# A new written order of the pieces, and new PSUM banks, in a transformer layer with routed experts

## The chip, the core and the metric

The kernel runs on one NeuronCore of a Trainium2 chip: one program, one launch. The time is the device time of the launch in microseconds (us), here the median of three runs. The core has five engines with a queue of instructions each: TensorE (PE in the profile; PEld is its weight load), VectorE (DVE), ScalarE (ACT), GpSimd (POOL) and SyncE (SP, which issues most of the transfers). Every engine takes its instructions strictly in the order written for it, and waits on semaphores for what the others make.

## The reference, cut to what matters

```python
h = layernorm(x) * (1 + ca) + sa                  # x: 8 x 1024 x 256, float32
q, k, v = split(h @ w_qkv)                        # 16 heads of 16
attn = softmax(where(causal, q @ k.T / 16, -1e30))
x = x + ga * ((attn @ v) @ w_o)
h = layernorm(x) * (1 + cb) + sb
shared = silu(h @ w1.T) * (h @ w2.T) @ w3.T       # hidden 1024
scores = sigmoid(h @ router_w.T)                  # 8 experts
gates = scores * (top 2 of scores + bias)
routed = sum over the 2 of  (silu(h1) * h2 * gate) @ w3[e].T
x = x + gb * (shared + routed)
```

`sa, ca, ga, sb, cb, gb` are six rows per batch element, made from `c` by a silu and a product with `wmod`.

## The kernel before, in words

The work is cut into **pieces**, and the order of all of them is written out by hand in the table `ORDER_OF` (from line 128): one list for each of the five kinds of batch, `first`, `second`, `loop`, `last` and `end`. The program runs `start`, then `first` (batch element 0), `second` (1), `loop` (2 to 6), `last` (7) and `end`. A batch computes the attention of element b and the shared feed-forward part of element b - 1; `end` computes the feed-forward part of element 7, all 71 expert tiles, and the output. `WORK` (line 336) holds the parsed lists. Each engine's program walks the same list (its function `batch`) and issues its own part of each piece, so that the list fixes the order on all five queues at once. It fixes nothing else: which semaphore a part waits for, and at which count, stands in the part's own function.

The pieces that the prediction speaks of, by name and number:

- `max:g:p` is the p-th of 18 blocks of q k products of a group of four heads, of which only the row maxima are wanted. TensorE (L1857) fills two PSUM banks, VectorE takes the maximum (`maxima`, L1338). For four of the 18 ScalarE copies the block (`copy_max`, L1130), GpSimd masks the copy (`select_max:g:p`, L941) and VectorE reduces it (`diag_max:g:p`, L1338). `shifts:g` and `max_turn:g` bring the maxima into the queries.
- `scores:t`, 80 a batch: TensorE (L1881) fills two banks, ScalarE takes the exponential (`exps`, L1148) into one of five buffers, which it must not write before `values:t-5` has read it; on the diagonal GpSimd masks it (L935).
- `values:t`: TensorE (L1903) adds up the products with v in one bank; `raw:n` and `normalise:n` finish a step on VectorE.
- `qk:g`, `v:h`, `turn:i`, `op:h`: projections and turns (L1831, L1843, L1819, L1981). `up:k:i` and `down:k:i` are the parts of the shared feed-forward (L1911, L1955), `hid:k` its way from fp32 to two fp16 halves.
- In `end`, for expert tile i (256 rows): `xr:i` lets VectorE work out gate and row numbers (L1550 to L1556), and lets SyncE issue the load of tile **i + 2** (`load_tile`, a transposing transfer at L740 and a small one at L742). `tup:i` is the tile's up projection: TensorE L1935, 24 matmuls into two banks, ScalarE's silu L1200, VectorE's product L1563. `tlo:i` splits the product (L1207, L1568). `ty:i` is the down projection: TensorE L1946, 12 matmuls into one bank, VectorE L1575, and two indirect stores by GpSimd (`add_tile`, L1017).
- Also in `end`: for each half m of a batch element `out_load:m` issues two loads on SyncE (base rows L754, 512 KB; the experts' sums L761, 1 MB), `out_make:m` is three VectorE operations of 128x1024 (L1581, L1590, L1592), `out_store:m` issues the store (L766). `out_load:0` waits for the stores of tiles 51 to 54; `out_load:m` from m = 2 on waits for `out_make:m-1` to be partly done, and from m = 4 on for `out_store:m-4` to have landed. `last_loads` and `out_end` do the same for the last four halves and wait for the last tiles.

PSUM has eight banks. `BANK_OF` (line 301) gives, as a row of digits for each kind of batch, the first bank of every use in the order of the list. The loop over `BATCHES` works out from it which earlier uses a piece's banks had last (`AFTER`), and TensorE's `take` (line 1809) waits until those were read (`was_read`, from line 1767). So a digit decides for which engine's work a piece waits.

## Time and profile before

| | us |
|---|---|
| median of three runs | 1887.2 |
| lowest and highest run | 1887.08, 1891.4 |
| the profiled execution, from its first to its last instruction (span) | 1884.2 |
| TensorE matmuls busy | 1724.3 |
| VectorE busy | 1581.7 |
| ScalarE busy | 1072.7 |
| GpSimd busy | 922.0 |

The profile is of one execution, whose own time is known only by its span. The median of the runs is 3.0 us above that span. Line numbers (L1881) are those of the kernel before. A matmul's end is modelled, so that two matmuls in a row seem to overlap; what a piece costs is better read as the distance from its first matmul to the first matmul of the next piece. The brackets at the end of a row give the idle time of the engine just before it, and what ended it.

### The profile page before, as it was taken

Reading aid. Unit: us, or ns where it says so; the run is one execution under the profiler, and the core shown is the slowest. Engines: PE = TensorE matmul, PEld = TensorE weight load, DVE = VectorE, ACT = ScalarE, POOL = GpSimd, SP = SyncE. Lnnn points to the kernel's source line nnn. Section 1 sums busy time; section 2 is a strip of 40 time slices with the busy share of each in tenths; the row PEclk is TensorE's granted clock in tenths of the full one; section 3 lists DMA queues with packets and bytes.
Section 4 is the critical chain, followed back from the end, with each engine's and each line's share of the span. In section 5 each row is a group of like instructions: output and inputs, shape, how many; then the busy total and the mean of one; then the engine's idle time right before and its main releaser. Section 6 shows DMA issues by size and latency. Waiting matters only on the chain. (4 is left out here: it accounts for less than half of the span.)

```text
span 1884.2 us, 46063 instructions
## 1 busy us (share of the span) xinstructions
PE 1724.3 (92%) x17630; PEld 984.1 (52%) x17630; DVE 1581.7 (84%) x2889; ACT 1072.7 (57%) x1346; POOL 922.0 (49%) x1003
## 2 busy tenths in 40 slices
PE   5677889999999999999999999999999998999987
PEld 2233435444554455445444545454545877778764
DVE  7999998898988898898889887988996676656787
ACT  2578767675766576667666765676575332323211
POOL 2233454455535554545545554545465376545423
PEclk8699999999999999999999999999999999999998
DMA  4236221303112312121212121213112775677998
GB/s 146 74 124 171 63 70 32 86 15 92 37 47 58 98 30 70 36 86 30 75 29 86 30 75 32 83 30 91 35 56 78 196 156 140 164 157 156 284 287 281
DMA packets 214132, 183.13 MB, mean 97 GB/s; under 512 B 146640, under 2 KB 182232, under 8 KB 212128
## 3 DMA queue, kind: packets, MB, share of 16 engines
q1 hardware_dynamic: 200768, 143.87, 29.6%
q0 software_dynamic: 12960, 36.06, 5.7%
q8 instruction: 146, 2.39, 0.5%
q14 instruction: 66, 0.54, 0.1%
q10 hardware_dynamic: 192, 0.26, 0.1%
HBM read 65.23 MB, written 62.19 MB: 68 GB/s over the span
## 5 line engine op out<-in xcount | busy, mean ns | idle before, releaser
L1148 ACT ACTIVATE arena<-pair 128x1024 f32<-128x1024 f32 (+1 forms) x640 | 569.3, 940 | 207.8 <-PE pair L1881 205.0
L1338 DVE TENSOR_REDUCE max_part<-pair 128x2 f32<-128x1024 f32 (+2 forms) x448 | 531.9, 1212 | 33.5 <-PE pair L1857 31.6
L1911 PE MATMUL pair<-feat_parts,ffn_sb 128*128 128x512 f16 x1536 | 379.4, 384 | 15.3 <-DMA feat_parts<-rows 5.0
L1903 PE MATMUL pair<-arena,v_sb 128*32 128x256 f32 (+1 forms) x5120 | 329.5, 368 | 5.1 <-POOL arena L935 1.0
L935 POOL TENSOR_SCALAR_AFFINE_SELECT arena<-arena 128x512 f32<-128x512 f32 x256 | 165.8, 658 | 265.7 <-ACT arena L1148 265.5
L1857 PE MATMUL pair<-arena 48*128 48x128 f16 (+3 forms) x2304 | 209.6, 282 | 39.8 <-DVE max_part L1338 14.7
L1881 PE MATMUL pair<-arena 50*128 50x256 f16 (+1 forms) x2560 | 208.4, 264 | 32.9 <-DVE silu_h L1386 7.9
L1911 PEld LDWEIGHTS pair<-feat_parts,ffn_sb 128*128 128x128 f16 x1536 | 133.7, 98 | 189.6 <-issue 38.5
L1017 POOL DMA_INDIRECT slots<-arena,feat x142 | 146.1, 1029 | 156.0 <-DVE arena L1575 127.5
L1023 POOL TENSOR_TENSOR hidden<-silu_h,hidden 128x512 f16<-128x512 f32 x128 | 149.8, 1172 | 147.7 <-ACT hidden L1181 147.0
L1935 PE MATMUL pair<-parts,arena 128*128 128x256 f16 x1704 | 201.7, 276 | 11.0 <-DMA parts<-lists 4.0
L941 POOL TENSOR_SCALAR_AFFINE_SELECT arena<-arena 128x1024 f32<-128x1024 f32 x128 | 141.7, 1107 | 127.5 <-ACT arena L1130 127.2
L1903 PEld LDWEIGHTS pair<-arena,v_sb 128*32 128x32 f32 x5120 | 130.6, 110 | 127.9 <-issue 64.0
L1955 PE MATMUL pair<-ffn_sb,hidden 128*128 128x256 f16 x1536 | 185.9, 274 | 3.2 <-POOL hidden L1023 3.2
L1935 PEld LDWEIGHTS pair<-parts,arena 128*128 x1704 | 166.6, 99 | 39.9 <-issue 15.5
L1881 PEld LDWEIGHTS pair<-arena 50*128 50x128 f16 x2560 | 86.9, 95 | 172.9 <-ACT arena L1148 43.4
L1857 PEld LDWEIGHTS pair<-arena 48*128 48x128 f16 x2304 | 83.5, 96 | 171.0 <-issue 43.5
L1955 PEld LDWEIGHTS pair<-ffn_sb,hidden 128*128 128x128 f16 x1536 | 145.4, 98 | 41.4 <-issue 14.5
L1130 ACT ACTIVATE arena<-pair 128x1024 f32<-128x1024 f32 x128 | 131.1, 1024 | 60.6 <-PE pair L1857 57.0
L1002 POOL DMA_INDIRECT lists<-rows,slot_now x128 | 127.4, 995 | 64.3 <-DVE slot_now L1482 35.5
L1338 DVE TENSOR_REDUCE max_part<-arena 128x8 f32<-128x1024 f32 x128 | 154.3, 1206 | 1.5 <-POOL arena L941 1.5
L1200 ACT ACTIVATE arena<-pair 128x512 f32<-128x512 f32 x71 | 42.4, 597 | 189.7 <-PE pair L1935 172.2
(219 smaller groups left out, 2165.8 us busy)
## 6 DMA issues: line engine op xcount, KB each, us to landing
arena<-parts SPq DMA_DIRECT2D x380, 64.0 KB, 2.3
rows<-x SPq DMA_DIRECT2D x8, 1024.0 KB, 5.6
x_sb<-x SPq DMA_DIRECT2D x16, 512.0 KB, 4.3
base<-norm SPq DMA_DIRECT2D x14, 512.0 KB, 3.7
ffn_parts<-hidden SPq DMA_DIRECT2D x8, 768.0 KB, 4.5
arena<-ffn_parts SPq DMA_DIRECT2D x8, 768.0 KB, 5.6
x_sb<-ffn_w SPq DMA_DIRECT2D x6, 768.0 KB, 6.4
norm<-ffn_w SPq DMA_DIRECT2D x6, 768.0 KB, 7.7
```

What stands on the lines that cost most here:

```text
L935: gp.affine_select(p, p, [[0, GH], [1, P]], ALU.is_ge, 0.0, 0, -1).then_inc(masked, 1)
L941: gp.affine_select(some, some, [[0, 2 * 4], [-1, P]], ALU.is_ge, NEG, 0, 1).then_inc(diag_masked, 1)
L1017: gp.indirect_dma_start(slot_dram, bass.IndirectOffsetOnAxis(ap=tile_id[i % 8][:, t:t + 1], axis=0), tile_out[i % 4][:, t, :], None).then_ ...
L1023: gp.tensor_tensor(hidden[:, 1, k % 8, :], silu_h[:, k % 2, :], hidden[:, 0, k % 8, :], ALU.subtract).then_inc(hidden_low, 1)
L1148: sc.activation(to[:, :, lo:QC], of[:, :, lo:QC], ACT.Exp, scale=SCALE / QK_SCALE ** 2).then_inc(exp_done, 1)
L1338: return vec.tensor_reduce(to, of, AX.X, ALU.max)
L1857: last = mm(to[:, 512 * s + at:512 * s + at + nk], q_stack[r, g, i, qt * P:(qt + 1) * P], k_stack[r, g, i, k0:k0 + nk], start=True, stop=True)
L1881: last = mm(to[:, at + lo:at + QC], k_stack[r, g, i, kt * P:(kt + 1) * P], q_stack[r, g, i, QC * c + lo:QC * (c + 1)], start=True, stop=True)
L1903: last = mm(to[32 * j:32 * j + 32, lo:QC], v_sb[:, kt, h:h + 32], probs[:, u % RING, at + lo:at + QC], start=(kt == 0), stop=(kt == 2 * c ...
L1911: last = mm(to[:, 0:512], w_up[s][W_PART[i]][:, f, m * RH + h * P:m * RH + (h + 1) * P], feat_parts[:, A_PART[i], f, c * 512:(c + 1) * 512 ...
L1935: last = mm(to[:, 512 * h + ROWS * m:512 * h + ROWS * (m + 1)], weights(W_PART[x] * UW + f * 2 * RH + m * RH + h * P, P), tile_feat[i % 4] ...
L1955: last = mm(to[:, 0:D], hidden[:, A_PART[i], j, t * P:(t + 1) * P], w_down[j // 2][W_PART[i]][:, j % 2, :], start=(i == 0 and j == 0), sto ...
```

## The change

Both tables are replaced for `first`, `second`, `loop`, `last` and `end`. In every kind of batch the new list holds exactly the same pieces, each once, in another order; the row of digits in `BANK_OF` is new too. No function, instruction, wait or buffer is changed (the waits of `take` follow from the banks). The diff is cut to the stretches of the lists that the prediction speaks of.

```diff
 ORDER_OF = {
     "first": """
-        max:1:0 max:1:1 max:1:2 max:1:3 max:1:4 share:0 max:1:5 share:1 select_max:1:1 diag_max:1:1
-        scores:0 qk:2 max:1:6 scores:1 scores:2 select_max:1:5 scores:3 values:0 values:1 raw:0 max:1:7 max:1:8 diag_max:1:5 max:1:9 max:1:10
+        max:1:0 max:1:1 max:1:2 max:1:3 max:1:4 diag_max:1:1 share:0 share:1 qk:2 select_max:1:1 scores:0 scores:1 max:1:5 values:0 select_max:1:5
+        select_max:1:10 max:1:6 raw:0 values:1 max:1:7 scores:2 scores:3 scores:4 max:1:8 diag_max:1:5 select_max:1:14 normalise:0 scores:5 scores:6 max:1:9
...
     "loop": """
-        scores:7 values:4 scores:8 values:5 values:6 max:1:11 select_max:1:10 scores:9 max:1:12 hid:-2 osp:2 raw:1 normalise:1 osp:3 values:7 values:8
-        values:9 max:1:13 diag_max:1:10 max:1:14 op:0 up:-1:0 rest:0 scores:10 up:-1:1 up:-1:2 scores:11 max:1:15
+        up:-2:5 raw:0 diag_max:1:5 max:1:9 max:1:10 scores:7 values:2 values:3 normalise:-1 scores:8 values:4 values:5 max:1:11 scores:9 max:1:12 values:6
+        values:7 max:1:13 diag_max:1:10 raw:1 select_max:1:10 op:0 rest:0 scores:10 scores:11 up:-1:0 up:-1:1 up:-1:2 up:-1:3 max:1:14 max:1:15 up:-1:4
...
     "end": """
-        ty:43 xr:47 tup:46 up:3:4 gate_rows tlo:45 tlo:46 ty:44 xr:48 tup:47 ty:45 ty:46 xr:49 tup:48 xr:50 tlo:47 tup:49 ty:47 xr:51 tlo:48 tup:50 ty:48
...
-        ty:54 xr:57 tup:56 tlo:55 xr:58 hid:3 tlo:56 tup:57 ty:55 xr:59 tup:58 tlo:57 tlo:58 ty:56 out_load:0 xr:60 tup:59 ty:57 tlo:59 out_load:1 xr:61
-        tup:60 ty:58 out_load:2 out_make:0 xr:62 tup:61 ty:59 out_load:3 tlo:60 out_make:1 up:4:0 up:4:1 up:4:2 tlo:61 up:4:3 up:4:4 up:4:5 up:5:0 up:5:1
-        up:5:2 hid:4 up:5:3 up:5:4 up:5:5 up:6:0 hid:5 out_store:0 out_store:1 xr:63 up:6:1 ty:60 up:6:2 up:6:3 up:6:4 up:6:5 up:7:0 out_load:4 out_make:2
...
-        up:12:1 up:12:2 up:12:3 up:12:4 up:12:5 hid:11 hid:12 up:13:0 up:13:1 up:13:2 up:13:3 up:13:4 up:13:5 up:14:0 up:14:1 up:14:2 out_store:11 last_loads
...
+        tlo:44 xr:46 tup:45 tlo:45 ty:43 xr:47 tup:46 ty:44 tlo:46 ty:45 xr:48 xr:49 tup:47 tup:48 hid:2 hid:3 ty:46 xr:50 tlo:47 tup:49 tlo:48 tlo:49 ty:47
...
+        xr:57 tup:56 ty:54 xr:58 tlo:55 tup:57 out_load:0 tlo:56 tlo:57 out_load:1 out_store:0 ty:55 xr:59 tup:58 tlo:58 ty:56 xr:60 tup:59 up:4:0 up:4:1
+        up:4:2 up:4:3 up:4:4 out_load:2 out_make:0 ty:57 tlo:59 xr:61 tup:60 out_make:1 out_load:3 out_make:2 tlo:60 ty:58 xr:62 tup:61 up:4:5 up:5:0 tlo:61
+        ty:59 out_make:3 ty:60 up:5:1 xr:63 tup:62 xr:64 up:5:2 tup:63 tlo:62 ty:61 tlo:63 out_store:1 up:5:3 up:5:4 up:5:5 out_store:2 up:6:0 up:6:1
...
+        out_load:10 up:14:2 out_load:11 hid:13 tlo:70 ty:67 ty:68 ty:69 up:14:3 up:14:4 up:14:5 ty:70 out_make:10 out_make:11 up:15:0 up:15:1 up:15:2 hid:14
+        hid:15 up:15:3 up:15:4 up:15:5 first_loads down:4:0 down:4:1 down:4:2 down:5:0 down:5:1 down:5:2 down:6:0 down:6:1 down:6:2 out_make:12 down:7:0
+        down:7:1 down:7:2 out_make:13 out_sum:14 out_tail:0 out_tail:1 out_store:9 out_store:10 out_store:11 out_tail:2 last_loads out_tail:3 out_end
+        out_sum:15 out_tail:4 out_tail:5 out_tail:6 out_tail:7
...
 BANK_OF = {
...
     "end": """
-        76040406146120410412046540401045062462045405404120420204020420420402040204042451420424056415265202502052505252502052505252542423424042404245
-        014152462565462747264232740434023252354054105400145
+        30426062402407402121510246003403246646007740305005642110227430640260416704627542406440400752446743435636460621062642264634741432503232243672
+        037262402450446404542440262327416610447535270652240
```

## Rows read from the trace of the kernel before

**Rows 1.** The page: busy time, and busy tenths in 40 slices of 47.1 us.
```profile
span 1884.2 us, 46063 instructions
...
PE 1724.3 (92%) x17630; PEld 984.1 (52%) x17630; DVE 1581.7 (84%) x2889; ACT 1072.7 (57%) x1346; POOL 922.0 (49%) x1003
...
PE   5677889999999999999999999999999998999987
...
DMA  4236221303112312121212121213112775677998
```

**Rows 2.** Busy us (instructions) by batch; then granted clock, DMA share, GB/s.
```profile
61.40:209.00 147.60, 118.63 (x1369) 51.51 (x1368) 138.37 (x189) 113.44 (x120) 46.19 (x50) 0.90 0.45 134
209.00:387.50 178.50, 164.14 (x1764) 80.24 (x1766) 161.01 (x278) 118.54 (x145) 91.80 (x101) 0.97 0.20 55
...
570.40:751.80 181.40, 173.93 (x1890) 89.97 (x1886) 161.70 (x289) 120.66 (x148) 95.84 (x104) 1.00 0.21 57
...
1301.40:1470.20 168.80, 165.59 (x1791) 86.52 (x1791) 137.96 (x272) 111.45 (x142) 91.28 (x102) 1.00 0.25 73
1470.20:1884.20 414.00, 372.71 (x3132) 300.41 (x3123) 288.03 (x641) 113.23 (x187) 199.86 (x195) 0.97 0.77 200
```

**Rows 3.** Timeline of TensorE from 302 us: start, us, line, operation, count.
```profile
302.79 0.86 PE L1903 MATMUL pair<-arena,v_sb 128*32 128x256 f32 x16
303.58 2.33 PE L1911 MATMUL pair<-feat_parts,ffn_sb 128*128 128x512 f16 x10
305.85 0.61 PE L1881 MATMUL pair<-arena 50*128 50x256 f16 x8
```

**Rows 4.** The page's groups: scores' exponential, row maximum, mask of a diagonal block.
```profile
L1148 ACT ACTIVATE arena<-pair 128x1024 f32<-128x1024 f32 (+1 forms) x640 | 569.3, 940 | 207.8 <-PE pair L1881 205.0
L1338 DVE TENSOR_REDUCE max_part<-pair 128x2 f32<-128x1024 f32 (+2 forms) x448 | 531.9, 1212 | 33.5 <-PE pair L1857 31.6
...
L941 POOL TENSOR_SCALAR_AFFINE_SELECT arena<-arena 128x1024 f32<-128x1024 f32 x128 | 141.7, 1107 | 127.5 <-ACT arena L1130 127.2
```

**Rows 5.** Timeline of the tile stage, TensorE, ScalarE and VectorE from 1704 us.
```profile
1705.51 5.40 PE L1935 MATMUL pair<-parts,arena 128*128 128x256 f16 x48
...
1708.39 0.60 ACT L1200 ACTIVATE arena<-pair 128x512 f32<-128x512 f32 x1 [4.64 <-PE pair L1935]
...
1709.02 0.69 DVE L1563 SCALAR_TENSOR_TENSOR arena<-pair,arena 128x512 f32<-128x512 f32 x1 [2.04 <-ACT arena L1200]
...
1711.03 1.53 PE L1946 MATMUL pair<-arena,feat 128*128 x12
...
1712.42 2.84 PE L1935 MATMUL pair<-parts,arena 128*128 128x256 f16 x24
1712.69 0.69 DVE L1575 TENSOR_TENSOR arena<-pair,feat 128x512 f32<-128x512 f32 x1 [0.37 <-PE pair L1946]
```

**Rows 6.** Timeline of TensorE, where the batch "end" loses time before 1570 us.
```profile
1547.58 1.61 PE L1946 MATMUL pair<-arena 128*128 x12 [1.93 <-DVE arena L1568]
...
1560.36 1.61 PE L1946 MATMUL pair<-arena 128*128 x12 [1.74 <-DVE arena L1575]
...
1568.47 0.17 PE L2018 MATMUL pair<-carry,ones 128*128 128x8 bf16 x1 [3.34 <-DVE carry L1472]
```

**Rows 7.** Output sums: landing times of the loads issued at L761.
```profile
DMA to landing us min/median/max: 5.5/8.7/11.7
```

**Rows 8.** VectorE timeline, first output half, after its load.
```profile
1760.22 1.23 DVE L1581 TENSOR_TENSOR feat<-feat 128x1024 f32<-128x1024 f32 x1 [2.95 <-DMA feat<-slots]
...
1762.81 1.23 DVE L1592 TENSOR_TENSOR feat<-feat,wqk_sb 128x1024 f32<-128x1024 f32 x1
```

**Rows 9.** The chain that ended last: start us, us, what it consists of.
```profile
1653.57 3.64 DMA parts<-lists
...
1848.47 7.30 DMA slots<-arena,feat
1855.92 7.41 DMA feat<-slots
```

More of the change, by code:

```diff
@@ L157 @@
+        values:72 values:73 scores:77 normalise:13 values:74 normalise:14 scores:78 scores:79 max_turn:0 values:75
     """,
     "second": """
[L159 to L161 removed]
@@ new lines @@
+        values:31 scores:32 rank:0 up:4:0 up:4:1 raw:6 scores:33 max:2:17 up:4:2 up:4:3 up:4:4 up:4:5 hid:4 scores:34 scatter:2 scatter:3 diag_max:2:14
+        shifts:2 rest:1 var:1 op:1 select_max:3:1 scores:35 scores:36 values:32 values:33 values:34 scores:37 up:5:0 max:3:0 max:3:1 up:5:1 up:5:2 values:35
+        max_turn:2 up:5:3 max:3:2 scatter:4 scores:38 up:5:4 up:5:5 up:6:0 table:0 up:6:1 up:6:2 up:6:3 hid:5 up:6:4 scores:39 max:3:3 up:6:5 scores:40
+        values:36 values:37 max:3:4 diag_max:3:1 max:3:5 normalise:6 scores:41 select_max:3:5 values:38 values:39 up:7:0 scores:42 scores:43 max:3:6 raw:7
```

293 lines of the change are left out of this document (133 added, 160 removed).

## The prediction

> **What bounds the kernel now.** First the page. TensorE's matmuls are busy 92% of the span, VectorE 84%, and the slices show TensorE at 90% or more from about 235 us to 1700 us; the transfers fill up only in the last four slices [rows 1]. An average over stages says little here, so I cut the span at the batches. The boundaries are found by laying TensorE's 17630 matmuls beside the lists, piece by piece. What to see [rows 2]: in `first` TensorE leaves 147.6 - 118.6 = 29.0 us idle while VectorE works 138.4 of 147.6 us, so VectorE sets the pace there. In `second` TensorE leaves 14.4 us, in a `loop` batch (five of them, between 181.4 and 184.8 us) 7.5 us, in `last` 3.2 us, in `end` 414.0 - 372.7 = 41.3 us. Inside `end` some 8 us go before 1570 us, where TensorE waits for VectorE's routing work [rows 6], and most of the rest after 1750 us, where the output halves and the last tiles share the transfer engines. The program ends on a chain of tile stores, sum loads and final sums [rows 9]. So in the middle a new order has little to win and can lose; in `end` it can do both.
>
> **The change, part by part.** All pieces stay. What moves is their order on all queues and the bank that each takes. I cost four things.
>
> *1. Changes of kind on TensorE.* Going on to a piece of another kind costs a little even where nothing is waited for. Ten matmuls of `up` start at 303.58 and take 2.33 us with the last one's length (about 0.38), so they follow each other at 0.216; ten of them are 2.16 us, and the next piece, of `scores`, starts 2.27 us after the first [rows 3]. That is 0.11 us for the change. From `tup` to `ty` it costs next to nothing: two `tup` and the start of `ty` lie 5.52 us apart, 48 matmuls at 0.115 [rows 5]. So I count changes between three groups, which use the array in different shapes: `max` and `scores` (48 or 50 rows), `values` (32 columns), all others. Over the program the old lists have 1228 of them and the new ones 1141: 20 fewer in `first`, 12 in `second`, 9 in each `loop`, 10 in `last`, none in `end`. 87 x 0.11 = 9.6: **-10 us**. Bounds: 0 and -15.
>
> *2. Banks taken again too soon, in the attention batches.* For each piece I add up the TensorE work that the list puts between the last use of its bank and its own start, with each piece at its shortest length (`up` 0.43, two pieces of `values` 0.79 [rows 3], `tup` 2.62, `ty` 1.39 [rows 5]), and compare it with what the reader of the bank needs. After `scores` that is the exponential, 0.94, after `max` the reduction, 1.21 [rows 4]; with 0.2 for the handovers I ask for 1.2 and 1.4 us. The missing microseconds add up, in the old order, to 36 in `first`, 9 in `second`, 7 in each `loop`, 4 in `last`. TensorE's real idle time there was 29.0, 14.4, 7.5 and 3.2 [rows 2], so the count is usable. In the new order it gives 48, 13, 4 and 3. I take `first` at half of its +12, since VectorE sets the pace there: +6 + 4 - 5 x 3 - 1 = **-6 us**. Bounds: -16 and +8.
>
> On the other queues little is due. In the new order GpSimd's `select_max` often stands ahead of its own `max` (in `loop`, `select_max:2:5` some 8 us ahead), so GpSimd waits there with diagonal masks queued behind it, and `values` behind those. GpSimd works 96 of 181 us in a `loop` batch [rows 2], and the distance from `scores` to `values` has grown (median 6.5 to 8.2 us); that covers it: 0. Without that cover each would cost up to a mask of 1.1 us [rows 4]. `scores:t` more often stands before `values:t-5` (ScalarE then waits for its buffer); by the lists this adds under 1 us a batch.
>
> *3. Banks in the tile stage of `end`.* Here the new order differs in kind. The old one has two pieces that come back to a bank too soon. The new one has 36. After `tup`, silu and product must be done: the first `tup` of the pair ends at 1705.51 + 2.62 = 1708.13, silu runs at 1708.39, the product ends at 1709.71, so 1.6 us are needed. After `ty`, which gives way at 1712.42, the product ends at 1713.38: 0.96 us [rows 5]. An instance: in `xr:48 xr:49 tup:47 tup:48` the digits give `tup:47` the bank of `ty:45`, the piece right before it. Ahead of `out_load:0` there are 14 pieces behind a `tup` (9.8 us missing), 9 behind a `ty` (8.6 us) and one other, together **+19 us**; before, 1 us. TensorE is the bound here (pieces follow without a gap [rows 5]), so nothing covers them. Bounds: 0, if TensorE had to wait at these places anyway, and +19. Against that stand the waits for the routing work, 1.93 + 1.74 + 3.34 = 7.0 us [rows 6]. The new list spreads `rank:1`, `count:1` and `table:1` over 31 us of tile work instead of under 1 us after `rank:1`: **-7 us** (bounds -8 and +3).
>
> The Trainium skill (Perfetto Trace Analysis, Matmul Optimizations) advises making use of all eight PSUM banks; in `end` the new digits do that better (banks 6 and 7 hold 28 and 30 uses, before 12 each). By that rule part 3 would be no loss, and the sum 19 us lower. The lists say otherwise: what counts is how soon a bank is taken again, and that is sooner.
>
> *4. The output part of `end`.* SyncE's queue is in order, and the new list puts `out_load:0` right behind tile 54, whose stores it waits for, then `out_store:0`, which waits for all of `out_make:0`, and only then the loads of tiles 61 and 62. From `out_load:0` to `tup:61` the list has 16 us of TensorE work. Needed are: the stores of tile 54, about 3; the load of the sums, 8.7 [rows 7]; three operations at 1.23, 3.7 [rows 8]; issues of about 2; the tile's landing, 3.6 [rows 9]. That is 21 us, 5 more. `out_make:2` then stands 4 us behind `out_load:2`, whose data need 8.7 us, and `ty:60` waits behind it on VectorE: again 5. Banks taken too soon after this point miss another 12 us, of which I count half, as they fall into waits that exist: 5 + 5 + 6 = **+16 us**. Nothing there can be won back by the fixed remainder: tiles 67 to 70 stand 12 us of TensorE work later in the list than before, and behind the last tile the chain still needs its stores (7.3), its loads (7.4) and the final sums [rows 9]. Bounds: 0 and +36 (12 for the late tiles, and 8 for stores 9 to 11, now sent with the last loads).
>
> **The sum.** -10 - 6 + 19 - 7 + 16 = +12 us against the span of 1884.2. The runs' median lies 3.0 us above that span, and I carry the difference over: 1887.2 + 12 = **1899 us**.
>
> **The rivals.** About 0.3% (5.7 us) is what a measurement of this kernel can tell from no change.
>
> *A, forecast:* the middle wins 16, `end` loses about 28. 1888 to 1912. Chance 0.46.
>
> *B, faster:* the short bank distances cost nothing, since TensorE waits at those places anyway for the tile's product or load. One mechanism, at the 36 places: it decides from the point where the input of the piece comes 1.0 to 1.6 us after the bank's last use. For it speaks that the old order fits the real waits of the middle batches so well that the new one, which improves there, may rest on as good an account of `end`; against it, that tile pieces follow each other without a gap before [rows 5]. Parts 3 and 4 then leave -7: -10 - 6 - 7 = -23, or 1864; with part 4's 10 us of transfers 1874. Chance 0.29. The skill's rule on the banks, above, would end here too.
>
> *C, no change:* `end` loses only the tile stage, +19 - 7, and that cancels the 16 of the middle: about 1883 to 1892. Chance 0.14.
>
> *D, much slower:* the output part takes its upper bound, 20 more than in A: 1919. For it speaks that the transfers are nearly full from 1740 us on [rows 1], so that time lost in issuing them is not made up. Chance 0.10.
>
> *E:* that the change does not do what it says. The lists hold the same pieces; 0.01.
>
> **How the numbers follow.** Faster is B, with its upper part and a little of C and E: 0.30. Same is C and the edge of A: 0.15. Slower is the rest, 0.55. The range goes from B's sum of 1864 to D's 1919; A's own is 1888 to 1912.
>
> **What would show it.** In the new profile: the `loop` batches 2 to 5 us shorter each (if they are not shorter, parts 1 and 2 fall); TensorE idle in `first` 29 us or more; in `end`, before 1750 us, waits of TensorE for L1563 and L1575, some 18 us together, where there were hardly any; a late load at L740 before tile 61; the last tile's stores more than 10 us later after the batch's start than before. I am wrong if `end` is not longer than 414 us: then the banks were covered (B). If `end` is longer but by the output alone, part 3 is wrong and part 4 too small.

## The result, and the profile after

The changed kernel takes 2013.8 us (median of 4 runs, 2007.6 to 2017.5) against 1887.8 us (the kernel before, median of 4 with a later run; the first three gave 1887.2): a ratio of 1.065, 95% interval 1.0623 to 1.0676. The direction was forecast, the size was not: +12 us forecast, +126 us measured, outside the range of 1864 to 1919 us.

In the code after the change every line behind the lists stands 19 lower: L1148 is L1129, L1338 is L1319, L1563 is L1544, L1575 is L1556.

The page of the changed kernel, the lines that answer to [rows 1]:

```profile
span 2012.5 us, 46079 instructions
...
PE 1754.7 (87%) x17630; PEld 1006.2 (50%) x17630; DVE 1638.7 (81%) x2889; ACT 1077.9 (54%) x1346; POOL 920.4 (46%) x1003
...
PE   5688899989998999899899989999898777897784
...
DMA  4245121212211221212131212221236455656866
```

Three things are to be seen. TensorE is at 9 in fewer slices from the first attention batch on, so the loss isn't in one place. VectorE is busy 57.0 us longer (1638.7 for 1581.7) with the same 2889 instructions. And the transfers, nearly full in the last slices before (9, 9, 8), now reach 8 in one slice only: how much they move isn't the limit.

By batch, the same windows as [rows 2]; the granted clock stands behind the last bracket:

```profile
61.70:221.70 160.00, 127.68 (x1371) 55.87 (x1370) 140.43 (x189) 114.17 (x120) 45.33 (x50) 0.81 0.42 123
221.70:397.60 175.90, 161.51 (x1763) 81.86 (x1766) 162.20 (x280) 119.18 (x145) 91.92 (x100) 0.97 0.19 52
...
583.25:770.90 187.65, 175.87 (x1886) 92.68 (x1882) 170.42 (x289) 121.50 (x148) 96.34 (x104) 0.97 0.21 55
...
1331.00:1508.50 177.50, 166.35 (x1795) 87.58 (x1795) 148.10 (x274) 111.86 (x142) 91.48 (x102) 0.99 0.23 71
1508.50:2012.50 504.00, 391.97 (x3131) 303.09 (x3123) 290.30 (x639) 112.88 (x187) 195.50 (x195) 0.92 0.62 164
```

Against [rows 2]: `first` +12.4, `second` -2.6, the five `loop` batches +3.9 each (mean 186.7 for 182.8) or +19.5, `last` +8.7, `end` +90. These make the 128 us between the spans. In `end` I cut further, at the first matmuls of four of its tiles (found by laying the matmuls beside the list): up to `ty:0`, to `ty:12`, to `ty:54`, to `ty:67`, and to the end of the span. Before 18.9, 47.4, 200.0, 96.1 and 51.5 us; after 18.3, 73.8, 227.4, 136.9 and 47.7. Below, the stretch from `ty:0` to `ty:12` is called the head. The new list has other amounts of TensorE's work in these stretches. With each piece at the shortest length that the trace of before shows, it does 5 us more of it between `ty:0` and `ty:12`, 2 less up to `ty:54`, 11 more up to `ty:67` and 14 less behind.

What TensorE waits for in `end` up to `ty:54` (engine, its line, what ended the wait: us in total, times, longest):

```profile
PE pair L1927 <- DVE arena L1549: 12.8, 7, 4.3
PE pair L1892 <- DVE arena L1544: 9.4, 3, 7.3
PE pair L1927 <- DVE arena L1544: 8.5, 6, 3.3
PE pair L1927 <- DVE feat L1549: 7.3, 2, 6.4
PE pair L1916 <- DVE arena L1556: 5.8, 5, 1.6
```

L1549 is the tile's own hidden rows, which `ty` needs as input. L1544 and L1556, waited for by a `ty`, an `up` or a `tup`, are readers of a bank that is to be taken again. So two causes are mixed: late input and late banks. Of these rows' 43.8 us, 12.5 (all for L1549) lie in the head, the rest behind `ty:12` but for 0.7.

A `loop` batch shows its main loss in one line, and the timelines of VectorE and GpSimd show why:

```profile
PE pair L1849 <- DVE max_bf L1341: 5.6, 2, 4.6
```

```profile
621.14 1.21 DVE L1319 TENSOR_REDUCE max_part<-arena 128x8 f32<-128x1024 f32 x1
622.44 0.32 DVE L1338 TENSOR_REDUCE max_row<-max_part 128x32 f32<-128x160 f32 x1
622.80 1.49 DVE L1340 TENSOR_SCALAR max_bf<-max_row 128x32 f16<-128x32 f32 x1
624.32 2.27 DVE L1341 SCALAR_TENSOR_TENSOR max_bf<-max_row,max_bf 128x32 f16<-128x32 f32 x1
```

```profile
622.13 2.12 POOL L966 TENSOR_TENSOR rows<-norm,rows 128x1024 f16<-128x1024 f32 x1 [4.14 <-ACT rows L1175]
624.21 2.34 POOL L1010 TENSOR_TENSOR x_sb<-x_sb,gates_sb 128x1024 f32<-128x1024 f32 x1
```

These are `shifts:1` on VectorE, which `max_turn:1` on TensorE needs. The new list has `shifts:1` behind `norm2:0:0` and `norm2:0:1`, and even behind `max_turn:1`, so it comes late; and its two short operations, 0.18 and 0.19 us elsewhere, last 1.49 and 2.27 us, each until GpSimd's operation ends. The Trainium skill (SBUF — State Buffer, Who interferes with whom) has this as a rule: VectorE and GpSimd share a pair of ports under an exclusive lock, taken by an operation of VectorE with two inputs in SBUF or in a two-port mode. The trace agrees as to L1341, which has two inputs in SBUF; L1340 has one, and that it ran in a two-port mode would fit its 1.49 us but isn't to be seen in the trace. L1338, a reduction with one input, runs inside GpSimd's operation from 622.13 us and keeps its usual 0.32 us.

### The profile page after: what moved, and what is told of

The parts are those of the page before. It is cut to its first block and busy times, and to the rows that moved or that the text cites. A ratio compares the mean times of both kernels' runs of the same rounds, so it can differ in the third digit from the quotient of the medians.

```text
span 2012.5 us, 46079 instructions
## 1 busy us (share of the span) xinstructions
PE 1754.7 (87%) x17630; PEld 1006.2 (50%) x17630; DVE 1638.7 (81%) x2889; ACT 1077.9 (54%) x1346; POOL 920.4 (46%) x1003
## 5 line engine op out<-in xcount | busy, mean ns | idle before, releaser
L1129 ACT ACTIVATE arena<-pair 128x1024 f32<-128x1024 f32 (+1 forms) x640 | 572.0, 938 | 214.3 <-PE pair L1862 194.1
L1319 DVE TENSOR_REDUCE max_part<-pair 128x2 f32<-128x1024 f32 (+2 forms) x448 | 532.7, 1214 | 41.1 <-PE pair L1838 37.6
L1892 PE MATMUL pair<-feat_parts,ffn_sb 128*128 128x512 f16 x1536 | 381.8, 386 | 25.6 <-ACT silu_h L1149 12.4
L998 POOL DMA_INDIRECT slots<-arena,feat x142 | 141.9, 999 | 208.2 <-DVE arena L1556 179.5
L1884 PEld LDWEIGHTS pair<-arena,v_sb 128*32 128x32 f32 x5120 | 140.8, 113 | 140.9 <-issue 69.0
L1936 PE MATMUL pair<-ffn_sb,hidden 128*128 128x256 f16 x1536 | 193.9, 281 | 12.2 <-POOL hidden L1004 10.9
L1862 PEld LDWEIGHTS pair<-arena 50*128 50x128 f16 x2560 | 91.9, 96 | 167.7 <-issue 52.1
L1111 ACT ACTIVATE arena<-pair 128x1024 f32<-128x1024 f32 x128 | 131.0, 1024 | 55.3 <-PE pair L1838 51.5
L1319 DVE TENSOR_REDUCE max_part<-arena 128x8 f32<-128x1024 f32 x128 | 154.2, 1205 | 0.2 <-POOL arena L922 0.2
```

The source lines that it names most:

```text
L998: gp.indirect_dma_start(slot_dram, bass.IndirectOffsetOnAxis(ap=tile_id[i % 8][:, t:t + 1], axis=0), tile_out[i % 4][:, t, :], None).then_ ...
L1129: sc.activation(to[:, :, lo:QC], of[:, :, lo:QC], ACT.Exp, scale=SCALE / QK_SCALE ** 2).then_inc(exp_done, 1)
L1319: return vec.tensor_reduce(to, of, AX.X, ALU.max)
L1862: last = mm(to[:, at + lo:at + QC], k_stack[r, g, i, kt * P:(kt + 1) * P], q_stack[r, g, i, QC * c + lo:QC * (c + 1)], start=True, stop=True)
L1884: last = mm(to[32 * j:32 * j + 32, lo:QC], v_sb[:, kt, h:h + 32], probs[:, u % RING, at + lo:at + QC], start=(kt == 0), stop=(kt == 2 * c ...
L1892: last = mm(to[:, 0:512], w_up[s][W_PART[i]][:, f, m * RH + h * P:m * RH + (h + 1) * P], feat_parts[:, A_PART[i], f, c * 512:(c + 1) * 512 ...
```

## The experiments

Each kernel is compared with the kernel before in runs on the same chip. The chips differ: on chips of kind A the kernel before took 1888 to 1891 us, on two others (kind B) 1952 and 1957, so ratios are compared, and batch times only within a kind. Batch times are those of one profiled execution of each kernel. The expectations call a bank a place.

### Is each batch's loss its own?

`e1_new_end` is the kernel before with `end` alone replaced, list and banks.

```diff
 ORDER_OF = {
...
-    "end": [list of before]
+    "end": [list of the change]
...
 BANK_OF = {
...
-    "end": [banks of before]
+    "end": [banks of the change]
```

> The kernel before with only the batch end (list and banks) from the changed kernel; start, first, second, loop and last as before. If what was lost sits inside each kind of batch, end costs here what it cost in the change, some +90 us, and the other batches keep their times: about 1978 us. If instead the end was longer because the batches ahead of it left work queued on VectorE and GpSimd, the end is clearly below its 504 us here (under 470) and the time is under 1950 us.

1979.4 against 1891.3 us, 1.0458 (1.0424 to 1.0493), kind A: +88. `end` took 499 us, for 504 in the changed kernel and 414 before. All but 5 us of its loss is its own.

### Banks

`e2_far_banks` keeps the new lists and deals all banks anew:

```diff
 BANK_OF = {
...
     "end": """
-        30426062402407402121510246003403246646007740305005642110227430640260416704627542406440400752446743435636460621062642264634741432503232243672
+        10246260742456024263245062672403456040610640465405640674045256405402623647607452046264026014270747274057202432606476420604120614021604104216
...
```

> The changed kernel's five lists word for word, with the PSUM places of all five dealt anew so that each is taken as late as possible: no place in the tile stage of end is taken within 1.6 us of its tup's end or 0.96 us of its ty's end (the changed kernel has 30 such). If short reuse of places is what the change lost (parts 2 and 3 of the prediction, carried further than they were priced), most of the 126 us goes: under 1930 us. If the order on the engines is what costs, it stays within 10 us of the prediction's own term for places, so 1990 to 2014 us: the 19 us of part 3 at most, and nothing else.

2063.8 us, 1.0904 (1.0862 to 1.0946), kind A: slower than the changed kernel, which no theory had. By parts it is clear in `end`, 477 us for 504: `ty:12` to `ty:54` took 207.3 us for 227.4, `ty:54` to `ty:67` 130.0 for 136.9, the head 74.9 for 73.8, so nothing. Banks are 20 us of the middle and 7 of the next stretch; `ty`'s wait for L1544 went from 19.7 us in all of `end` to 2.6. But each `loop` took 197.7 us for 186.7, `second` 185.2 for 175.9 and `last` 189.2 for 177.5.

`e4_near_banks` goes the other way: the lists of before, only the row of `end` changed.

```diff
 BANK_OF = {
...
     "end": """
-        76040406146120410412046540401045062462045405404120420204020420420402040204042451420424056415265202502052505252502052505252542423424042404245
+        76266666646666666666666666666774656665666665222622222222222222222222222222272676622226466544666666666666666666666666666664444444444444444447
...
```

> The kernel before, lists word for word, with the places of end's tup and ty pieces dealt so that each takes the place left last: by nominal durations 136 of them in the tile stage are taken 145 us too soon in sum, where the changed kernel has 30 with 26 us. If a short reuse costs what it lacks (part 3 of the prediction), end is 145 us longer: about 2030 us. If a short reuse costs a part of that because TensorE gets it back from slack further on, the added time over 145 us is the share by which part 3 was mispriced; if it costs nothing, 1888 us.

2081.9 us, 1.100 (1.0957 to 1.1043), kind A, `end` 609 us for 414. The waits are the two that the theory names:

```profile
PE pair L1927 <- DVE arena L1544: 72.8, 46, 2.3
PE pair L1916 <- DVE arena L1556: 46.0, 44, 2.1
PE pair L1916 <- DVE arena L1544: 29.6, 18, 3.0
```

195 us for 145 missing by the count: short distances cost all that they lack and a third more. The three rows make 148 us; where the rest arises wasn't taken apart. This is an order in which TensorE waits for little else. In the new order, where rival B says that the input is late anyway, `e2_far_banks` decides: with the list unchanged the distances cost 20 us of the tile stage. B is out.

Why were far banks worse in the attention batches? `e12_far_again` mends the loop (below) and counts the distance from the reader's piece in the list, `e16_far_by_reader` adds an allowance for the reading itself.

Both take all of `BANK_OF` anew, and their list of `loop` is that of `e3_loop_shifts_out`. A bank counts as free in `e2_far_banks` when its owner's last write has ended, in `e12_far_again` when the reader's piece has its place in the list as well, in `e16_far_by_reader` 3.5 us after that for maxima, 1.6 for scores and 2 to 4 for others:

```diff
 BANK_OF = {
...
-    [the banks of all five kinds in the change]
+    [dealt anew: each piece takes the bank that has been free the longest]
```

> All five lists of the changed kernel, with the mended loop of e3_loop_shifts_out, and the places of all kinds dealt as late as possible, late now counting from the reader's point in the list too. e2_far_banks counted from the writing's end alone and made each loop 11 us longer though no place was taken soon by that count. If a place behind an accumulator is held until the piece that reads it (raw, rest, place) comes up in its engine's queue, the loops are now 178 to 183 us on a chip like the first, and the ratio 1.035 to 1.045. If it is the change of places itself that costs (a matmul that changes its place), they stay at 190 us or more, and the ratio above 1.06.

> As e12_far_again (all lists of the change, mended loop), with late places counted from the expected end of the reading: the writing's end plus 3.5 us where VectorE reads maxima, 1.6 us where ScalarE reads scores, 2 to 4 us for the rest. e12's loops were 192 us on the second kind of chip, where the same lists with the changed kernel's own places had 187.5. If unequal readers are why places far from the writing did worse, the loops come to 186 to 189 us. If they stay at 191 us or more, a place's distance is not what its own row of places gets right, and that stays open.

`e12_far_again`: 1.0627 (1.0548 to 1.0706), kind B, loops 192.4 us, where the same list with its own banks has 187.5 on that kind (`e5_best_kinds`). `e16_far_by_reader`: 1.0748 (1.0716 to 1.0779), kind A, loops 192.3, where it has 181.0 (`e3_loop_shifts_out`). Both theories miss: the loops stay 5 and 11 us longer. What the trace of `e16_far_by_reader` has, in one loop, and that kernel (`e3_loop_shifts_out`) hasn't:

```profile
PE pair L1838 <- ACT arena L1129: 4.3, 8, 0.8
PE pair L1862 <- ACT shift_rows L1119: 2.1, 1, 2.1
PE pair L1892 <- ACT arena L1129: 2.0, 3, 1.0
```

Maxima and `up` wait for ScalarE's exponentials, that is, for banks that `scores` left. My reading, which no run isolates, is that a piece then meets a reader whose queue is longer than the fixed allowance; why the row that came with the list does better stays open. In `end` the far deal kept its gain (206.3 us from `ty:12` to `ty:54` in `e16_far_by_reader`).

### The displaced piece in `loop`

`e3_loop_shifts_out` moves two pieces of VectorE back, and in `end` the output's pieces to the point of TensorE's work where the old list has them:

```diff
 loop:
-        scores:16 down:-4:1 norm2:0:0 norm2:0:1 down:-4:2 down:-3:0 down:-3:1 values:12 diag_max:1:14 values:13 values:14 halves:0 max_turn:1 scores:17 ln:0 shifts:1
+        scores:16 down:-4:1 diag_max:1:14 shifts:1 norm2:0:0 norm2:0:1 down:-4:2 down:-3:0 down:-3:1 values:12 values:13 values:14 halves:0 max_turn:1 scores:17 ln:0
```

> The changed kernel with two edits that touch no TensorE piece and no place. In loop the two VectorE pieces diag_max:1:14 and shifts:1 are moved ahead of norm2:0:0 (in the changed list shifts:1 stands behind the max_turn:1 that needs it). In end the loads, sums and stores of the output stand at the same point of TensorE's work as in the list of before. Theory of the queue order: the 4.6 us wait of max_turn in each of five loop batches goes, the loops come out 3 to 5 us shorter each, and end's stalls behind out_make and the tile loads go, 20 to 40 us of its +90: 1950 to 1975 us in all. Theory of the places: neither edit touches a place, so it stays at 2005 to 2014 us.

1985.8 us, 1.0492 (1.0445 to 1.0539), kind A: 28 us below the changed kernel. Nearly all of it is in the loops: mean 181.0 us for 186.7, less than the 182.8 of before. One of them, and what is left of the wait:

```profile
759.20:939.90 180.70, 172.03 (x1888) 91.13 (x1884) 165.10 (x289) 120.99 (x148) 96.06 (x104) 1.00 0.22 58
```

```profile
PE pair L1849 <- DVE max_bf L1341: 1.2, 1, 1.2
```

TensorE is also 3.8 us less busy than in the changed kernel's loop, at a granted clock of 1.00 for 0.97: the pause cost clock too. The half of the edit in `end` gave nothing (504 us either way).

The reverse, one displacement put into the kernel before: `e14_shifts_late`. `e15_no_collision` also takes GpSimd's piece out of its way.

```diff
 loop of before:
-        max:1:16 max:1:17 qk:2 down:-4:0 down:-4:1 values:11 select_max:1:14 diag_max:1:14 shifts:1 norm2:0:0 norm2:0:1 raw:2
+        max:1:16 max:1:17 qk:2 down:-4:0 down:-4:1 values:11 select_max:1:14 norm2:0:0 norm2:0:1 raw:2
         scores:14 scores:15 scores:16 down:-4:2 values:12 scores:17 values:13
-        halves:0 normalise:2 max_turn:1
+        diag_max:1:14 shifts:1 halves:0 normalise:2 max_turn:1
```

The last line is that of `e14_shifts_late`; in `e15_no_collision` it reads:

```diff
+        diag_max:1:14 shifts:1 normalise:2 max_turn:1 halves:0
```

> The kernel before with one displacement of the change put into its loop alone: diag_max:1:14 and shifts:1 of VectorE behind norm2:0:0, norm2:0:1 and raw:2, right ahead of GpSimd's halves:0. TensorE's list is untouched. If this is what made the changed loops long (in e3_loop_shifts_out undoing it gave 6 us a loop), max_turn:1 waits 3 to 6 us in each of five loops and the kernel is 15 to 30 us longer, ratio 1.008 to 1.016. If before's own order has slack that covers it: under 1.003.

> As e14_shifts_late, with GpSimd's halves:0 moved behind max_turn:1, so that VectorE's two short operations of shifts:1 no longer run beside it. In the changed kernel these took 1.5 and 2.3 us for 0.2 each, ending with GpSimd's operations. If GpSimd's hold on VectorE is a part of the cost, these are back at 0.2 us and the loops 3 to 4 us shorter than in e14_shifts_late. If the place in the list alone costs, both kernels have the same loops within 1 us.

1.0127 (1.0098 to 1.0157) and 1.0116 (1.0042 to 1.019), kind A. The loops: 188.4 us in `e14_shifts_late`, 186.9 in `e15_no_collision`, 182.8 before. L1340 over one batch in each (count, then min, median, max in ns):

```profile
L1340 DVE TENSOR_SCALAR max_bf<-max_row x4: 181/182/1455, 803.4 to 941.5; 128x32 f16<-128x32 f32 x4
```

```profile
L1340 DVE TENSOR_SCALAR max_bf<-max_row x4: 181/181/183, 804.9 to 941.0; 128x32 f16<-128x32 f32 x4
```

and TensorE's wait at L1849 in the two:

```profile
PE pair L1849 <- DVE max_bf L1341: 4.4, 1, 4.4
```

```profile
PE pair L1849 <- DVE max_bf L1341: 3.1, 1, 3.1
```

So the displacement costs 5.6 us a loop. In `e14_shifts_late` TensorE is also busy 176.5 us in this batch, at a granted clock of 0.98, for 173.9 at 1.00 before, with the same pieces: about half of the loss is clock. By the mean of five loops in one profile each, 1.5 us are GpSimd's hold on VectorE (the wait falls by 1.3, L1340 was 1.27 too long) and the rest is the place in the list, both with their share of clock; the times of the two kernels lie too close to tell them apart. In the changed kernel the hold is larger: L1340 and L1341 together last 3.4 us longer than elsewhere, in a wait of 4.6. What moving GpSimd's pieces alone gives there wasn't run.

### `end`: queues, single pieces, stretches

`e8_end_far` is the kernel before with the new list of `end` and far banks. `e6_end_queues` also puts the pieces that feed SyncE and GpSimd (`close`, `pads`, `scatter`, `table_rest`, `gate_rows`, all output pieces) where TensorE's work stood in the old list.

```diff
 "end" of BANK_OF, first line, in e8_end_far:
-        76040406146120410412046540401045062462045405404120420204020420420402040204042451420424056415265202502052505252502052505252542423424042404245
+        76240206142450640425401624234065012605250162505265062760250642504506267243203456042624062014630343634053606476202432460204160214061204104612
 "end" of ORDER_OF, one stretch, in e6_end_queues:
-        tlo:23 tup:24 up:0:3 up:0:4 table:1 ty:22 xr:26 tup:25 scatter:12 scatter:13 up:0:5 ty:23 xr:27 close:0 tlo:24 scatter:14 scatter:15 tlo:25 tup:26 ty:24 pads xr:28
+        tlo:23 tup:24 up:0:3 up:0:4 table:1 ty:22 xr:26 tup:25 pads table_rest:1:0 up:0:5 ty:23 xr:27 tlo:24 tlo:25 tup:26 ty:24 xr:28
```

> The kernel before with end's list from the changed kernel and end's places dealt as late as possible, late now meaning the later of the writing's end and the point in the list at which the reader's piece stands. The one before this (far places in all kinds) took TensorE's part of end from 487 to 460 us. Theory: places are 27 us of end's +88, the rest is the order on VectorE, GpSimd and SyncE: 1948 to 1955 us. If the reader's point matters as well, up to 15 us less: 1935 us.

> As e8_end_far, and the pieces of end that only issue transfers or only feed SyncE and GpSimd (close, pads, scatter, table_rest, gate_rows and the output's loads, sums and stores) stand where TensorE's work stood in the list of before. The theory of the queues (tile loads held on SyncE behind close and out_load, VectorE held by xr behind them) says that most of what is left of end goes: 1905 to 1925 us. The theory that the order of tup, ty, tlo and hid among themselves is what costs says that it stays within 10 us of e8_end_far.

1.0297 (1.0259 to 1.0335) and 1.0286 (1.0238 to 1.0334), kind B. The first leaves +60 of `e1_new_end`'s +88, as expected for banks. The second falls as a theory: the transfers' place isn't what costs. In the profiles `end` took 501.2 us for 504.3, with the stretch from `ty:54` to `ty:67` 6 us shorter and the head 3 us longer.

`e11_three_steps` mends the three largest single stalls of `e8_end_far`:

```diff
-        norm2:0:0 norm2:0:1 tup:4 op:1 ty:2 tlo:4 xr:6 ty:3 xr:7 ty:4 tup:5 rest:1 halves:0 ln:0 var:1
+        norm2:0:0 norm2:0:1 halves:0 ln:0 tup:4 op:1 ty:2 tlo:4 xr:6 ty:3 xr:7 ty:4 tup:5 rest:1 var:1
-        xr:10 tup:9 xr:11 tup:10 tlo:9 tlo:10
+        xr:10 tup:9 tlo:9 xr:11 tup:10 tlo:10
-        ty:70 out_make:10 out_make:11 up:15:0 up:15:1 up:15:2 hid:14 hid:15 up:15:3 up:15:4 up:15:5 first_loads
+        ty:70 up:15:0 up:15:1 up:15:2 hid:14 hid:15 up:15:3 up:15:4 up:15:5 out_make:10 out_make:11 first_loads
```

> As e8_end_far, with four pieces of VectorE, ScalarE, GpSimd and SyncE moved, none of TensorE's: halves:0 and ln:0 ahead of tup:4 (they stood right behind rest:1, whose addition of two arrays of SBUF then lasted 5.7 us for 1.2), tlo:9 ahead of tup:10, and out_make:10 and 11 behind up:15:5 (they held VectorE 7.4 us ahead of the last silu product). Theory of the single queue mistakes: the stalls of 6.1 us before ty:5, 4.5 before ty:9 and 8.5 before down:4:0 go, 12 to 19 us less than e8_end_far's +60: a ratio of 1.020 to 1.025. If something else is late right behind each, under 5 us come back: 1.028 or more.

1.0277 (1.0176 to 1.0377), kind B: an interval too wide for the question, but in the profile `end` took 506.1 us for 504.3, so nothing came back, and two of the stalls show what was late next. At the first, in the changed kernel, an addition of two arrays of SBUF on VectorE held up by two operations of GpSimd:

```profile
1547.71 5.74 DVE L1398 TENSOR_TENSOR x_sb<-x_sb,norm 128x1024 f32<-128x1024 f32 x1
```

```profile
1547.92 2.15 POOL L966 TENSOR_TENSOR rows<-norm,rows 128x1024 f16<-128x1024 f32 x1
1550.01 2.35 POOL L1010 TENSOR_TENSOR x_sb<-x_sb,gates_sb 128x1024 f32<-128x1024 f32 x1
```

In `e11_three_steps` that addition takes 1.23 us, as it should. But `halves:0` is now ScalarE's next piece ahead of `tup:4`'s silu, and `ty:2` waits 4.9 us there instead. At the last stall the silu product of `up:15` is now done at 1966.5 us, yet the down pieces start at 1974.6. GpSimd's queue in `e11_three_steps`:

```profile
1960.48 0.99 POOL L998 DMA_INDIRECT slots<-arena,feat  x1 [1.43 <-DVE arena L1556]
1961.77 0.96 POOL L998 DMA_INDIRECT slots<-arena,feat  x1 [0.30 <-issue]
...
1970.13 0.96 POOL L998 DMA_INDIRECT slots<-arena,feat  x1 [0.30 <-issue]
1971.10 3.39 POOL L1004 TENSOR_TENSOR hidden<-silu_h,hidden 128x512 f16<-128x512 f32 x2
```

```profile
1974.64 1.65 PE L1936 MATMUL pair<-ffn_sb,hidden 128*128 128x256 f16 x7 [8.90 <-POOL hidden L1004]
```

`ty:67` to `ty:70` come in one cluster in the new list. Each makes GpSimd issue two additions, 1.27 us apart, so eight of them stand ahead of the last hidden rows. `e13_tiles_early` moves three of the four:

```diff
-        tup:69 up:10:1
+        tup:69 ty:67 up:10:1
...
-        up:11:0
+        ty:68 up:11:0
...
-        up:13:3
+        up:13:3 ty:69
...
-        tlo:70 ty:67 ty:68 ty:69 up:14:3
+        tlo:70 up:14:3
```

> Two kinds of batch of the changed kernel in the kernel before, each with one thing mended. end: as e11_three_steps, and ty:67, 68, 69 (TensorE, VectorE and GpSimd each) stand 7, 5 and 2 tiles' worth of other work earlier, so that GpSimd issues their additions (two a tile, 1.27 us each) before hid:14 and hid:15 and not right ahead of them. If that queue on GpSimd is what held the last down pieces once VectorE was out of the way, the 8.9 us wait before down:4:0 falls under 4 us; if not, it stays at 8 or more. first: only qk:2 is moved, to its place of before (behind max:1:6). If qk:2 ahead of the first scores is what left TensorE idle and its clock low for 20 us longer, first falls from 159 to 165 us to under 154; if not, it stays.

1.0391 (1.0331 to 1.0451), kind A, with `end` and `first` both new. The wait is now short, and GpSimd has two issues ahead:

```profile
1917.64 0.99 POOL L998 DMA_INDIRECT slots<-arena,feat  x1 [4.41 <-DVE arena L1556]
1918.94 0.96 POOL L998 DMA_INDIRECT slots<-arena,feat  x1 [0.30 <-issue]
1919.92 1.17 POOL L1004 TENSOR_TENSOR hidden<-silu_h,hidden 128x512 f16<-128x512 f32 x1
```

```profile
1923.33 3.02 PE L1936 MATMUL pair<-ffn_sb,hidden 128*128 128x256 f16 x19 [3.53 <-POOL hidden L1004]
```

The mechanism is shown; but `ty:67` itself then waited 7.2 us, and `end` took 478.9 us, where far banks alone gave 477.2 on that kind (`e2_far_banks`). Single mistakes can be named one by one, and those mended here gave nothing in sum.

Whole stretches can be tested instead. `e10_head_old` has the pieces ahead of `ty:12` in the order of before, `e9_ends_old` those from `ty:54` on as well; the sets of pieces are the new list's, banks far.

```diff
 "end" of ORDER_OF, in e10_head_old:
-    [new list up to ty:12]
+    [the same pieces, in the old order]
     [new list from ty:12]
 and in e9_ends_old also:
-    [new list from ty:54]
+    [the same pieces, in the old order]
```

> The kernel before with an end whose middle alone is new: the pieces that the changed list has ahead of ty:12 stand in the order of before, the pieces from ty:54 on too, those between as in the changed kernel; places as late as possible. If the loss beyond the places lies in the order of these two stretches (ty:0 to ty:12 took 74 us for 47, ty:54 to ty:67 137 for 96), both come back and the kernel is within 0.5% of before (ratio 1.000 to 1.006). If the new middle passes its backlog on, or a stretch is only as good as its neighbour, the ratio stays above 1.012.

> As e9_ends_old, but only the first stretch of end (ahead of ty:12) is in the order of before, all the rest as in the changed kernel; places as late as possible. By the stretches this keeps the loss from ty:54 on, some 31 us of e8_end_far's 60: a ratio of 1.016 to 1.020, with ty:0 to ty:12 at 47 to 50 us and ty:54 to ty:67 at 125 to 130 us. If the first stretch's loss merely moves back (it did 5 us more of TensorE's work), ty:12 to ty:54 is some 5 us longer than in e8_end_far.

`e10_head_old` 1.0233 (1.0126 to 1.0341), `e9_ends_old` 1.0070 (1.0048 to 1.0092), kind B. The head fell from 72.8 us (`e8_end_far`) to 59.7; I had expected 47 to 50 and overlooked that it does 5 us more work. The stretch from `ty:54` to `ty:67` fell from 128.9 (`e10_head_old`) to 92.5, and what follows grew from 48.2 to 53.8. With both old, some 46 of the 60 us are gone. So in `end`: banks 27, the order of the last part some 31, of the head 13 or more, and a rest of some 14, of which 8 to 12 are seen from `ty:12` to `ty:54` (237.3 us; with the unchanged list 224.9 and 229.0 in two kernels on that kind). Which pieces of these orders cost what stays open but for the ones named above.

### `first`, `last`, and a version that beats both

`e7_select_late` moves every `select_max` that stands ahead of its own `max` right behind it, eight in `first`, three in `last`:

```diff
-        qk:2 select_max:1:1 scores:0 scores:1 max:1:5 values:0 select_max:1:5 select_max:1:10 max:1:6 raw:0
+        qk:2 select_max:1:1 scores:0 scores:1 max:1:5 values:0 select_max:1:5 max:1:6 raw:0
```

> The kernel before with first and last from the changed kernel, and in both each select_max that stands ahead of its own max (eight in first, three in last) moved right behind it. Part 2 of the prediction had the early select_max at no cost: then first stays at 159 to 162 us and last at 175 to 178 us, 1908 to 1912 us in all. If GpSimd, waiting in one of them, holds back the diagonal masks that values wait for, first comes out under 155 us and last under 173 us, 1895 to 1903 us.

1.0096 (1.0059 to 1.0133), kind B; `first` 160.5 us, `last` 179.5 where `last` of before takes 170 on that kind. `first` and `last` keep their losses, so the early `select_max` costs nothing that is seen here; the lists without this edit weren't run on that kind of chip, and a gain of a microsecond or two would not show. `qk:2` back in its old place didn't help either (`e13_tiles_early`: `first` 158.7).

`e18_first_head_old` takes `first` and `second` from the change and the rest from before, with the head of `first`, up to `max_turn:1`, in the old order, each piece with its new bank; its first line:

```diff
-        max:1:0 max:1:1 max:1:2 max:1:3 max:1:4 diag_max:1:1 share:0 share:1 qk:2 select_max:1:1 scores:0 scores:1 max:1:5 values:0
+        max:1:0 max:1:1 max:1:2 max:1:3 max:1:4 share:0 max:1:5 share:1 select_max:1:1 diag_max:1:1 scores:0 qk:2 max:1:6 scores:1
```

> The kernel before with first and second from the changed kernel, and in first the pieces ahead of max_turn:1 (the first 43 us of the batch, in which the changed kernel's TensorE waited 16 us and had a granted clock of 0.6 to 0.8) in the order of before, each with the changed kernel's place. If that stretch is where first loses its 12 us, first takes 148 to 152 us; second 174 to 178 us as before. If the loss lies behind it, first stays at 158 us or more.

1.0078 (1.0044 to 1.0112), kind A; `first` 165.9 us, longer still. `max_turn:1` starts 43.7 us into the batch in the changed kernel, 47.9 here, and at 31.0 before. Some 4 us of the 12.7 are work done ahead (`mods`, which the old list has behind it); the rest of the batch doesn't give them back, as it takes 116.3 us, before 116.6. So some 9 of the 12 us are lost in this head. The first 43 us, before and after:

```profile
61.40:105.00 43.60, 36.09 (x371) 14.26 (x370) 39.92 (x54) 33.69 (x36) 11.36 (x15) 0.80 0.38 117
```

```profile
61.70:105.00 43.30, 32.42 (x261) 12.10 (x261) 33.67 (x35) 27.13 (x27) 8.13 (x10) 0.66 0.30 92
```

TensorE gets through 261 matmuls for 371, at a granted clock of 0.66 for 0.80. Old order with new banks does no better, so here the banks are under suspicion, and the trace of `e18_first_head_old` from 61.7 us to its `max_turn:1` at 109.6 points there too, with `scores` waiting for the readers of the maxima's banks:

```profile
PE pair L1862 <- DVE max_part L1319: 9.0, 3, 3.4
```

The new order with old banks wasn't tried. The cause in `first` stays open, and so does that in `last`.

Two kernels look for a better mix. `e5_best_kinds` is the kernel before with `second` of the change and the mended `loop` (the change's, with the two displacements of `e3_loop_shifts_out` undone), `e17_mended_loop` has the mended `loop` alone:

```diff
 ORDER_OF and BANK_OF, in e5_best_kinds alone:
-    "second": [list and banks of before]
+    "second": [list and banks of the change]
 and in both:
-    "loop": [list and banks of before]
+    "loop": [list of e3_loop_shifts_out, banks of the change]
```

> The kernel before with two kinds of batch taken from the changed kernel: second as it stands there, and loop with diag_max:1:14 and shifts:1 ahead of norm2:0:0. By the batch times seen so far second is 1 to 3 us shorter than before's, and the mended loop 181.0 against 182.8 us, five times: 1875 to 1880 us, a ratio of 0.993 to 0.996. If the rival holds that a batch's time depends on the order of the batch ahead of it, the gain is lost at the two seams (first to second, loop to last): 1888 us.

> The kernel before with one kind of batch from the changed kernel: loop, with diag_max:1:14 and shifts:1 ahead of norm2:0:0. Its batches took 181.0 us in e3_loop_shifts_out for 182.8 of before, but in e5_best_kinds the batch last behind them was 6 us longer than behind before's loops. If both hold, five times 1.8 less and 6 more: 3 us less, a ratio of 0.997 to 1.000. If the seam belonged to that kernel's second batch or its chip, 9 us less: 0.994 to 0.996, and this is the version that beats both.

`e5_best_kinds`: 1.0014 (0.9983 to 1.0044), kind B, no difference, where 0.993 to 0.996 was expected; its loops were 187.5 us where unchanged ones on that kind are 188.6 to 189.8, but `second` took 183.0 for 176 to 182 and `last` 175.5 for 170. `e17_mended_loop`: 1886.2 against 1889.8 us, **0.9976 (0.9960 to 0.9993)**, kind A. It beats both kernels, by little. In its profile the loops take 181.9 us in the mean and `last` 172.6 for 168.8, so the seam takes back about 4; but the profiled execution was the slowest of the twelve (1890.6 us), so these parts don't show the gain.

## Why the prediction was wrong

By kind of batch the terms of the sum say +4 for `first`, +3 for `second`, -20 for the five loops, -2 for `last` and +28 for `end`. Measured were +12, -3, +19.5, +9 and +90.

*The steps that held.* Part 3's bank term: +19 us forecast for the tile stage, 20 measured between `ty:12` and `ty:54` (`e2_far_banks`), with the two waits named. Rival B, that short distances cost nothing, is refuted by that run in the new order and by `e4_near_banks` in the old. The advice of the Trainium skill to make use of all eight banks (Perfetto Trace Analysis, Matmul Optimizations) does not decide it either way: the change uses the eight more evenly and loses these 20 us, and `e2_far_banks` uses all eight too and wins them back. Part 1 and the bank count of part 2 had the right sign for `loop`: once mended, a loop is 1.8 us shorter than before (0.9 in `e17_mended_loop`), for 4.0 forecast (1.0 and 3.0), so half at most. The early `select_max` costs nothing, as said. For `second` their sign was wrong: 2.6 us shorter.

*Part 2's "on the other queues little is due".* This is the step that failed first, a term put at nothing. I compared TensorE's list with itself and looked on the other queues at two kinds of piece. I never asked, for each piece that TensorE waits for, where its maker stands in its own queue. In `loop` `shifts:1` is written behind the `max_turn:1` that needs it, and behind `norm2`. That cost 5.7 us in each of five batches (186.7 to 181.0 when undone, and 5.6 when put into the kernel before); +19.5 measured for the loops where -20 stood in the sum. The distance on TensorE even looked better: 16.4 us from the last maximum to `max_turn:1`, of which 4.6 are the wait, before 9.0.

*Part 3 has no term for the order in `end`'s tiles.* Its -7 was for waits that lie behind `ty:12` before (1547 to 1568 us). The largest of them, the 3.34 us of `count:1`, is indeed gone. But the head, ahead of it, which the sum has at nothing, became 26 us longer, of which 5 is work done ahead. In it TensorE waits 12.5 us for the tiles' own hidden rows (L1549), before 1.4. With the old order 13 us came back (`e10_head_old`), so the order costs at least that; `halves:0` right behind `rest:1`, and `tlo` behind the next tile's product, are places where it shows, but moving these alone gave nothing (`e11_three_steps`).

*Part 4.* Its terms were +16, upper bound +36; the stretch from `ty:54` to `ty:67` cost 41 - 11 for work done ahead, and what follows gives back 4 where its work is 14 less: some 40 in sum. The late `out_load`, on which the 5 + 5 us rested, is 6 of it at most (`e6_end_queues`, and the half of `e3_loop_shifts_out`). The order of this last part as a whole is some 31 (`e9_ends_old` against `e10_head_old`). The clusters, VectorE's output sums and GpSimd's eight additions ahead of a product that the next matmuls wait for, are a part of it that is seen, but undoing them gave nothing in sum. The bank share was right (6 forecast, 7 measured).

*The clock.* It stands nowhere in the sum. In `first` I took half of a bank count, +6, for idle time; idle rose 3.3 us, but TensorE was busy 9.0 us longer at a granted clock of 0.81 for 0.90 [rows 2]. `end` has 19 us more busy time at 0.92 for 0.97.

*The range.* Its upper end added one term's bound. All five kinds of batch were rewritten, and an order on the other queues that I hadn't looked at was more likely to add waits than to take them away; with `loop` counted five times that needed a far wider upper side.

## What to carry to other kernels

When an order written out by hand changes, check it per engine: for every wait of the bounding engine, take the work queued on the maker's own engine ahead of the piece that ends it, and let pieces in a loop body count by their repeats. A bank taken again too soon can cost all that it lacks and more, but dealing all banks far can cost more than it gains. Keep short VectorE operations that TensorE waits for clear of long GpSimd ones. Count what stands in GpSimd's queue ahead of a product that TensorE waits for: eight issues of 1.27 us each made a wait of 8.9 us here, two one of 3.5. And mend in stretches: one stall removed often only shows the next.

## What the runs showed of the hardware

- A VectorE operation of 0.2 to 1.2 us can last 1.5 to 5.7 us beside GpSimd. In the changed kernel 93 operations lasted over 0.15 us longer than the median of their line and shape, 80 us in sum; before, 49 with 28 us. All of them overlap an operation of GpSimd. That is 52 us more, nearly all of the 57 by which VectorE is busier. What is seen in TensorE's waits is far less: in a `loop` batch, the one at `max_turn:1`.
- GpSimd's issues of indirect transfers take 0.96 us each and follow each other at 1.27 us (`e11_three_steps`).
- With a pause of 4.4 us put into a batch in which TensorE is otherwise busy, the granted clock over the batch is 0.98 for 1.00, and TensorE is busy 2.6 us longer with the same matmuls (`e14_shifts_late`).
- The same program differs by 3.3% and more between chips, and not evenly. With unchanged lists a loop takes 182.8 us on one kind and 188.7 on the other (`e7_select_late`), and `ty:12` to `ty:54` 200.0 and 224.9 (`e5_best_kinds`), the latter at granted clocks of 0.97 and 0.94. Why wasn't tested.
